# A scan layer's coefficients made in its projection phase, and block 0's spread weights picked out by TensorE

## The chip, the cores and the metric

The kernel runs on one core of one Trainium2 chip. The metric is the device time of one execution, in microseconds. Before the change the median of three runs is 3763.84 us (3762.84 to 3764.57).

## The reference

Four residual layers run one after the other on x (32 batches, 128 steps, 512 channels). Layers 1 and 2 are attention layers, which the change doesn't touch. Layers 0 and 3 are scan layers, each with weights of its own:

```
xr, gate = split(x @ W_in.T)                      # 1024 channels each
xc = silu(conv4(xr + t_emb) + b_conv)             # causal, one filter a channel
xn = layernorm(xc) * ln_g + ln_b
Bm, Cm, dt = split(xn @ W_xproj.T)                # 16 columns each
dt = tanh(dt @ W_dt.T + b_dt) * 0.01
Ad = 1 - dt * tanh(A_log)
Bd = Bm * minimum(norm(xn), 1)
h = clip(h * Ad[t] + Bd[t] * xn[t], -10, 10)      # 128 steps, 16 x 1024 a batch
y[t] = sum over the 16 states of Cm[t] * h
x = x + ((y + D * xn) * silu(gate)) @ W_out.T
```

## The kernel before

A scan layer is two phases with a barrier between them. Tiles named l0a and l3a belong to the projection phase of layers 0 and 3, l0r and l3r to the recurrence phase, l0s and l3s are kept over both. Inside a phase each engine works through its own instructions in order, and semaphores tie the engines together; SyncE (SP) and ScalarE (ACT) each have a queue of DMA issues of their own, and an issue that waits holds up all issues behind it on that engine.

**Projection (project_phase).** Eight tiles of four batches (512 tokens). SP loads W_in in 16 chunks of 512 columns; between the chunks it issues the small loads of a list, `loads`, one or two at a time. fold_dt (line 367, TensorE) multiplies W_dt into W_xproj as soon as all of `loads` have landed. VectorE evacuates the projected channels with t_emb added (line 616, tile l0a_pad), convolves them (line 627), and normalises; TensorE multiplies xn by W_xproj, and VectorE keeps the 48 columns of each token (line 658, l0s_proj). GpSimd makes the skip term D*xn (line 748), whose rows go to DRAM (dx_s); xn goes there split in a high and a low half (xhl_s), and so does the gate (gate_s). SP issues the last of these stores at line 286.

**Recurrence (recurrence_phase).** The state stands on 128 partitions of 8 batches x 16 states, for four groups of batches (GJ = 4), 1024 channels. A custom instruction of VectorE makes one step of one group (line 1196), so 512 make the scan; they are taken in 32 blocks of four steps. The recurrence is scaled by the running product `prod` of Ad: the feed is Bd/prod, the clip's bounds are 10/prod and -10/prod, and the reader's columns are Cm*prod. All that is made at the head of the phase, out of l0s_proj: VectorE removes the mean and applies the deviation for all 48 columns of all tokens in four products (lines 1155 to 1159), takes the three parts apart, waits for GpSimd's square root of the norms (line 911, a power), TensorE turns the parts so that steps lie along a row, ScalarE takes tanh, VectorE scans the product (line 1171), takes its reciprocal (1172), and makes the feed (1176), the bounds and the reader's columns. TensorE turns the feed back (line 996), ScalarE and VectorE split it (1100, 1180), and SP stores both halves to DRAM (feed_s, lines 844 and 846).

**Spread weights.** For each block SP loads the feed's rows from there, repeated over the partitions (line 852, l0r_crow, two loads of 256 KB a block), and GpSimd multiplies them by a mask `same` into block diagonal weights (line 922, l0r_wv). With those TensorE spreads xn over states and batches (line 1005, l0r_pv), the input of the steps. It reads a pair of steps out with the reader's columns (line 1020, l0r_py); ScalarE copies the sum out of PSUM (keep_y, line 1105, l0r_y), GpSimd adds the skip term and multiplies by the gate, and TensorE multiplies by W_out.

**Order at the recurrence's head.** SP issues x for blocks 0 and 1 (line 859, eight loads, which wait for the stores of the phase before), dx and gate of block 0, the feed's two stores, waits for both, then the spread rows of blocks 0 and 1, then W_out in eight chunks through two staging buffers (line 895): chunk c waits until chunk c-2 has been used. ScalarE casts a chunk (line 1125, l0r_woh), GpSimd makes its low half (line 970, l0r_wol). ScalarE's first keep_y comes behind the eight castings. TensorE's order for a pair of steps is spread, then read-out of the pair before; a read-out into l0r_py waits until ScalarE has copied the one before.

```
                        load_x(0, 0)
                        load_x(1, 1)
                        load_tokens(0, 0)
                        store_feed()
                        load_feed(0, 0)
                        load_feed(1, 1)
```

## Time and profile before

| what | value |
|---|---|
| median of three runs | 3763.84 us |
| the profiled execution | 3766.1 us |
| its span | 3764.3 us |
| mean granted TensorE clock | 0.963 |
| TensorE, VectorE busy | 3412.0 us (91%), 2965.0 us (79%) |
| GpSimd, ScalarE busy | 1868.6 us (50%), 1355.2 us (36%) |

The span is the time from the first to the last instruction of the profiled execution. The busy shares are means over layers that have different limits: the attention layers lie in the middle of the span, the scan layers at its ends. A timeline row gives the start from the span's start, the length, the engine (PE is TensorE, DVE VectorE, POOL GpSimd, SPq and ACTq the DMA issues of SyncE and ScalarE), the line, the operation, the tiles and how many equal instructions stand in the row; in brackets is how long the engine was idle before, and what released it.

### The profile page before, as it was taken

Reading aid. Unit: us, or ns where it says so; the run is one execution under the profiler, and the core shown is the slowest. Engines: PE = TensorE matmul, PEld = TensorE weight load, DVE = VectorE, ACT = ScalarE, POOL = GpSimd, SP = SyncE. Lnnn points to the kernel's source line nnn. Section 1 sums busy time; section 2 is a strip of 40 time slices with the busy share of each in tenths; the row PEclk is TensorE's granted clock in tenths of the full one; section 3 lists DMA queues with packets and bytes.
Section 4 is the critical chain, followed back from the end, with each engine's and each line's share of the span. In section 5 each row is a group of like instructions: output and inputs, shape, how many; then the busy total and the mean of one; then the engine's idle time right before and its main releaser. Section 6 shows DMA issues by size and latency. Waiting matters only on the chain. (4 is left out here: it accounts for less than half of the span.)

```text
span 3764.3 us, 62060 instructions
## 1 busy us (share of the span) xinstructions
PE 3412.0 (91%) x22068; PEld 2260.9 (60%) x22068; DVE 2965.0 (79%) x3172; ACT 1355.2 (36%) x2078; POOL 1868.6 (50%) x1384
## 2 busy tenths in 40 slices
PE   7999839999996899999999999997999948999998
PEld 6777614444443667777777777775777733444444
DVE  4777769999996777777778777763576769999998
ACT  3555512221222553444444444432455522122121
POOL 2555645655563024444454444433355655556554
PEclk9999959999998899999999999998999968999999
DMA  4566765565554224222322222224466675555553
GB/s 128 217 259 257 271 239 203 203 219 214 200 215 142 80 72 138 85 82 78 111 96 87 80 83 85 74 63 133 162 259 237 257 294 196 217 201 210 216 206 136
DMA packets 288573, 631.00 MB, mean 168 GB/s; under 512 B 33472, under 2 KB 35904, under 8 KB 288224
## 3 DMA queue, kind: packets, MB, share of 16 engines
q1 hardware_dynamic: 281200, 615.49, 46.6%
q10 hardware_dynamic: 7104, 11.81, 0.9%
q8 instruction: 183, 3.00, 0.3%
q14 instruction: 86, 0.70, 0.1%
HBM read 390.75 MB, written 241.70 MB: 168 GB/s over the span
## 5 line engine op out<-in xcount | busy, mean ns | idle before, releaser
L1196 DVE CUSTOM_DVE_ANT_0 l0r_g<-l0r_g,l0r_pv,l0r_cf 128x1024 f32<-128x1024 f32 x512 | 641.9, 1336 | 20.6 <-PE l0r_pv L1005 19.0
L1196 DVE CUSTOM_DVE_ANT_0 l3r_g<-l3r_g,l3r_pv,l3r_cf 128x1024 f32<-128x1024 f32 x512 | 641.8, 1337 | 17.8 <-PE l3r_pv L1005 16.2
L137 PE MATMUL l1h_ps_p<-l1h_xh,l1c_wh 128*128 128x512 f32 x768 | 323.3, 421 | 5.6 <-issue 3.3
L139 PE MATMUL l1h_ps_p<-l1h_xl,l1c_wh 128*128 128x512 f32 x768 | 306.3, 399 | 0.0
L138 PE MATMUL l1h_ps_p<-l1h_xh,l1c_wl 128*128 128x512 f32 x768 | 304.9, 397 | 0.0
L2182 POOL TENSOR_TENSOR l1h_st<-l1h_veps 128x1 f32<-128x1 f32 x64 | 35.4, 554 | 530.5 <-DVE l1h_veps L2040 530.5
L1794 ACT ACTIVATE l1h_pt<-l1h_ps_t 128x512 f32<-128x512 f32 x256 | 151.4, 591 | 330.7 <-PE l1h_ps_t L1667 330.7
L1020 PE MATMUL l0r_py<-l0r_g,l0r_cd 128*32 128x512 f32 x2048 | 253.1, 613 | 1.3 <-ACT l0r_y L1105 1.3
L1020 PE MATMUL l3r_py<-l3r_g,l3r_cd 128*32 128x512 f32 x2048 | 252.0, 611 | 0.8 <-ACT l3r_y L1105 0.8
L2080 DVE TENSOR_TENSOR l1h_e<-l1h_e,l1h_mx 128x1024 f32<-128x1024 f32 x128 | 207.2, 1619 | 4.4
L2099 DVE TENSOR_TENSOR l1h_vt<-l1h_ps_p,l1c_dc 128x512 f32<-128x512 f32 x64 | 44.3, 691 | 194.6 <-PE l1h_ps_p L139 194.6
L1005 PE MATMUL l0r_pv<-l0r_x,l0r_wv 32*128 32x512 f32 x1024 | 132.3, 503 | 50.6 <-DVE l0r_g L1196 29.7
L1787 ACT ACTIVATE l1h_e<-l1h_e 128x1024 f32<-128x1024 f32 x128 | 134.9, 1054 | 118.8 <-DVE l1h_e L2023 117.5
L1005 PEld LDWEIGHTS l0r_pv<-l0r_x,l0r_wv 32*128 32x128 f32 x1024 | 53.5, 185 | 206.3 <-issue 137.0
L1005 PE MATMUL l3r_pv<-l3r_x,l3r_wv 32*128 32x512 f32 x1024 | 131.4, 499 | 50.5 <-DVE l3r_g L1196 29.4
L1005 PEld LDWEIGHTS l3r_pv<-l3r_x,l3r_wv 32*128 32x128 f32 x1024 | 53.2, 184 | 205.8 <-issue 136.8
L627 DVE SCALAR_TENSOR_TENSOR l3a_pacc<-l3a_pad,l3a_wconv,l3a_pacc 128x512 f32<-128x512 f32 x192 | 144.8, 754 | 34.6 <-ACT l3a_pacc L485 30.1
L627 DVE SCALAR_TENSOR_TENSOR l0a_pacc<-l0a_pad,l0a_wconv,l0a_pacc 128x512 f32<-128x512 f32 x192 | 144.8, 754 | 34.1 <-ACT l0a_pacc L485 29.5
L2207 POOL TENSOR_TENSOR l1h_vl<-l1h_vt,l1h_vh 128x512 fp32r<-128x512 f32 x64 | 123.7, 1933 | 92.2 <-ACT l1h_vh L1825 92.2
L1667 PE MATMUL l1h_ps_t<-l1h_ident,l1h_e 128*128 128x128 f32 x1024 | 161.8, 281 | 6.4 <-ACT l1h_pt L1794 5.6
L139 PEld LDWEIGHTS l1h_ps_p<-l1h_xl,l1c_wh 128*128 128x128 f32 x768 | 145.9, 190 | 36.2
L137 PEld LDWEIGHTS l1h_ps_p<-l1h_xh,l1c_wh 128*128 128x128 f32 x768 | 146.4, 191 | 33.6 <-issue 4.3
(400 smaller groups left out, 8965.1 us busy)
## 6 DMA issues: line engine op xcount, KB each, us to landing
l0r_x<-xhl_s SPq DMA_DIRECT2D x128, 512.0 KB, 5.9
l3r_x<-xhl_s SPq DMA_DIRECT2D x128, 512.0 KB, 5.7
xhl_s<-l0a_xo SPq DMA_DIRECT2D x116, 512.0 KB, 4.6
xhl_s<-l3a_xo SPq DMA_DIRECT2D x116, 512.0 KB, 4.6
gate_s<-l0a_gate SPq DMA_DIRECT2D x64, 256.0 KB, 3.0
l0r_dx<-dx_s SPq DMA_DIRECT2D x32, 512.0 KB, 7.7
l0r_gate<-gate_s SPq DMA_DIRECT2D x32, 512.0 KB, 8.6
l0r_crow<-feed_s SPq DMA_DIRECT2D x64, 256.0 KB
```

Of the source, the lines that this page charges most:

```text
L137: pe.matmul(out, wh, xh, start=first, stop=False)
L138: pe.matmul(out, wl, xh, start=False, stop=False)
L139: return pe.matmul(out, wh, xl, start=False, stop=last)
L627: dve.scalar_tensor_tensor(out=a, in0=pad[:, it % 2, :, c:c + S], scalar=wconv[:, it, c:c + 1], in1=a, op0=ALU.mult, op1=ALU.add).then_inc ...
L1005: last = pe.matmul(pv[(k.off + t + 2 * p + a) % 3][:, h * HALF:(h + 1) * HALF], wv[r, k.parity(), 2 * t + p, :], x[r, k.parity(), t, p, :] ...
L1020: last = pe.matmul(py[j * JW:(j + 1) * JW, :], cd[:, k.parity(), t, j, at:at + JW], g[:, t, j, h * HALF:(h + 1) * HALF], start=t % 2 == 0 ...
L1196: dve._custom_dve(bass.dve_ops.TENSOR_ADD_SAT, out=g[:, t, j, :], in0=g[:, (t - 1) % TS, j, :], in1=pv[(k.off + t + j) % 3][:, :], s0=cf[: ...
L1667: last = pe.transpose(ps_t[:, h * S:(h + 1) * S], e[:, k.mod(2), u // 2, h, u % 2, :], ident[:, :])
L1787: act.activation(e[:, k.mod(2), half, :, :, :], e[:, k.mod(2), half, :, :, :], ACT.Exp).then_inc(exp_ok, 1)
L1794: act.activation(pt[:, u % 2, :, :], ps_t[:, :].rearrange("p (h s) -> p h s", h=HG), ACT.Copy).then_inc(pt_ok, 1)
L2080: dve.tensor_tensor(block, block, total.unsqueeze(3).to_broadcast([P, HG, 2, S]), ALU.mult).then_inc(en_ok, 1)
L2207: pool.tensor_tensor(vl[:, n.mod(2), :, :], vt[:, n.parity(), :, b * S:(b + 1) * S], vh[:, n.mod(2), :, :].bitcast(F32), ALU.subtract).the ...
```

## The change

Three things move, in both scan layers.

- **The coefficients.** Normalising the columns of dt and of Bm, turning them, tanh, the running product, its reciprocal and the feed are made at the end of the projection phase. The feed and the product are kept in `carry`, a tile that takes the place of l0a_pad; the intermediate values stand in the projection's xc tile. The columns of dt come first, then those of Bm; those of Cm stay in the recurrence. GpSimd's square root of the norms is split in 28 columns, between its last two skip terms, and 4 behind the last one.
- **The constants.** same, ymask, A_log and a new array `comb` are kept over both phases and are loaded by SP as the last four of `loads`; ScalarE's loads at the recurrence's head are gone, and so is the second load of ident.
- **Block 0's weights.** The spread rows of block 0 are no longer loaded. GpSimd makes two tiles of picks from comb and ident; TensorE multiplies the split feed by them in 16 matmuls, and VectorE multiplies the sum by `same`. The feed's store to DRAM and block 1's load remain. Rows of even blocks now come into `carry`, those of odd blocks into l0r_crow. GpSimd clears g in place of VectorE.

```diff
+                 (drow[:, :], w["D"].partition_broadcast(P)),
+                 (same[:, :], cst["same"]),
+                 (ymask[:, :], cst["ymask"]),
+                 (comb[:, :], cst["comb"]),
+                 (alog[:, :], w["A_log"].rearrange("(a n b) -> a n b", a=1, b=1).to_broadcast([GB, NS, 1]))]
...
+            for c, part in enumerate((steps, gains)):
+                pe.wait_ge(ready, c + 1)
+                for j in range(GJ):
+                    last = pe.transpose(ptr[:, c * TW + j * S:c * TW + (j + 1) * S], part[:, j * P:(j + 1) * P], ident[:, :])
+                last.then_inc(swung, 1)
...
+            act.wait_ge(summed, 1)
+            act.activation(acol[:, 0:1], alog[:, :], ACT.Tanh).then_inc(tanh, 1)
+            act.wait_ge(swung, 1)
+            act.activation(decay.rearrange("p j s -> p (j s)"), ptr[:, 0:TW], ACT.Tanh).then_inc(tanh, 1)
...
+            def normalise(c, m, out):
+                cols = slice(c * NS, (c + 1) * NS)
+                chain(dve.tensor_tensor(m, stat[:, :, 0].unsqueeze(2).to_broadcast(wide),
+                                        wsum[:, cols].unsqueeze(1).to_broadcast(wide), ALU.mult))
+                chain(dve.tensor_tensor(m, proj[:, :, cols], m, ALU.subtract))
+                chain(dve.tensor_tensor(m, m, stat[:, :, 2].unsqueeze(2).to_broadcast(wide), ALU.mult))
+                return dve.tensor_tensor(out, m, wbias[:, cols].unsqueeze(1).to_broadcast(wide), ALU.add)
...
+            dve.wait_ge(proj_ev, NT)
+            dve.wait_ge(rstd, B)
+            normalise(2, means[0], steps.rearrange("p (b n) -> p b n", b=B)).then_inc(ready, 1)
+            rows_b = gains.rearrange("p (b n) -> p b n", b=B)
+            chain(normalise(0, means[1], rows_b))
+            dve.wait_ge(root, 2)
+            chain(dve.tensor_scalar(norm[:, :], norm[:, :], 1.0, None, ALU.min))
+            dve.tensor_tensor(rows_b, rows_b, norm[:, :].unsqueeze(2).to_broadcast(wide), ALU.mult).then_inc(ready, 1)
+            chain(dve.memset(zero, 0.0))
+            dve.wait_ge(tanh, 2)
+            chain(dve.tensor_scalar(acol[:, 1:2], acol[:, 0:1], -0.01, None, ALU.mult))
+            chain(dve.tensor_scalar(decay, decay, acol[:, 1:2], 1.0, ALU.mult, ALU.add))
+            for j in range(GJ):
+                chain(dve.tensor_tensor_scan(prod[:, j, :], decay[:, j, :], zero, 1.0, ALU.mult, ALU.add))
+            inv = proj[:, :, 0:NS]
+            chain(dve.reciprocal(inv, prod.rearrange("p j (a b) -> p (j a) b", b=NS)))
+            dve.wait_ge(swung, 2)
+            chain(dve.tensor_tensor(feed.rearrange("p j (a b) -> p (j a) b", b=NS), ptr[:, TW:2 * TW].rearrange("p (a b) -> p a b", b=NS),
+                                    inv, ALU.mult))
...
+            def lengths(lo, hi):
+                pool.wait_ge(ss, hi)
+                pool.tensor_tensor(norm[:, lo:hi], stat[:, lo:hi, 3], half[:, :].to_broadcast([P, hi - lo]), ALU.pow).then_inc(root, 1)
...
                 if n >= B - TB:
                     skip_term(n)
+                if n == B - 2:
+                    pool.wait_ge(summed, 1)
+                    pool.memset(half[:, :], 0.5).then_inc(halved, 1)
+                    pool.wait_ge(halved, 2)
+                    lengths(0, B - TB)
+            lengths(B - TB, B)
...
+        rows_of_feed = (carry[:, 0:2 * TS * P].rearrange("p (a i) -> p a i", i=P), crow[:, :, :])
+        PICK = P + HALF_P
+        picks = [z.rearrange("p e m i -> p (e m i)")[0:32, GJ * P:GJ * P + PAIR * PICK].rearrange("p (t n) -> p t n", t=PAIR) for z in (zh, zl)]
...
-                at_least(sp, wvm, k - 1)
+                at_least(sp, wvm, k - 2)
+                if q == 0 and isinstance(k, int):
+                    sp.wait_ge(coefs, 3)
                 for h in range(2):
-                    sp.dma_start(crow[h * 64:(h + 1) * 64, q, :, :].rearrange("p a i -> p (a i)"),
+                    sp.dma_start(rows_of_feed[q][h * 64:(h + 1) * 64, :, :].rearrange("p a i -> p (a i)"),
...
                         store_feed()
-                        load_feed(0, 0)
                         load_feed(1, 1)
...
-            pool.memset(half[:, :], 0.5).then_inc(root, 1)
-            pool.wait_ge(root, 1)
-            pool.tensor_tensor(norm[:, :], stat[:, :, 3], half[:, :].to_broadcast([P, B]), ALU.pow).then_inc(root, 1)
-            for r in range(2):
-                pool.wait_ge(sent[1][r], 64 * B // 2)
+            for c in range(2):
+                pool.tensor_tensor(picks[c], comb[:, :].unsqueeze(1).to_broadcast([32, PAIR, PICK]),
+                                   ident[0:32, PAIR * c:PAIR * c + PAIR].unsqueeze(2).to_broadcast([32, PAIR, PICK]), ALU.mult).then_inc(pick, 1)
+            for q in range(2):
+                pool.wait_ge(sent[1][q], 64 * B // 2)
+                pool.wait_ge(sent[2][q], 16 * B // 2)
             pool.memset(cd[:, :, :, :, :], 0.0).then_inc(zeroed, 1)
+            pool.memset(g[:, TS - 1, :, :], 0.0).then_inc(gup, GJ)
             pool.wait_ge(zeroed, 1)
-            pool.wait_ge(same_ld, 32)
-            pool.wait_ge(step, 8 + 3 + GJ + 1 + 3)
+            pool.wait_ge(coefs, 3)
...
                         bounds(0, 0)
-                        weigh(0, 0, 1)
                         readers(0, 0)
                     if not (last and q == 1):
                         bounds(k + 1, 1 - q)
-                        weigh(k + 1, 1 - q, i + 1 + q)
+                        weigh(k + 1, 1 - q, i + 1)
...
-            pe.wait_ge(const, 16)
-            pe.wait_ge(step, 8)
-            for c in range(3):
-                for j in range(GJ):
-                    last = pe.transpose(pt[c][:, j * S:(j + 1) * S], parts[c][:, j * P:(j + 1) * P], ident[:, :])
-            last.then_inc(turned, 1)
-            pe.wait_ge(fed, 1)
             for j in range(GJ):
                 last = pe.transpose(pf[:, (j % 2 * 2 + j // 2) * P:(j % 2 * 2 + j // 2 + 1) * P], feed[:, j, :], ident[:, :])
             last.then_inc(feed_turned, 1)
+            pe.wait_ge(read_ready, 1)
+            for j in range(GJ):
+                last = pe.transpose(pc[:, j * S:(j + 1) * S], reads[:, j * P:(j + 1) * P], ident[:, :])
+            last.then_inc(read_turned, 1)
+            pe.wait_ge(pick, 2)
+            for c, half in enumerate((feed_h, feed_l)):
+                pe.wait_ge((feed_high, feed_low)[c], 1)
+                for t in range(TS):
+                    for e in range(2):
+                        last = pe.matmul(pv[2][:, t * 2 * P:(t + 1) * 2 * P], picks[t // PAIR][:, t % PAIR, HALF_P - 32 * e - 16 * c:HALF_P - 32 * e - 16 * c + P], half[0:32, 2 * e:2 * e + 2, :],
+                                         start=c == e == t % 2 == 0, stop=c == e == t % 2 == 1)
+            last.then_inc(picked, 1)
...
-                pe.wait_ge(wvm, k.count(1, 1))
+                at_least(pe, wvm, k.count())
+                if k.is_at(0):
+                    pe.wait_ge(first_w, 1)
...
-            act.dma_start(ident[:, :], cst["ident"]).then_inc(const, 16)
-            for b in range(GB):
-                act.dma_start(alog[b * NS:(b + 1) * NS, :], w["A_log"].rearrange("(n a) -> n a", a=1)).then_inc(alog_ld, 16)
-            act.dma_start(same[:, :], cst["same"]).then_inc(same_ld, 16)
-            act.dma_start(ymask[:, :], cst["ymask"]).then_inc(same_ld, 16)
-            act.wait_ge(alog_ld, 16 * GB)
-            act.activation(acol[:, 0:1], alog[:, :], ACT.Tanh).then_inc(tanh, 1)
-            act.wait_ge(turned, 1)
-            act.activation(decay.rearrange("p j s -> p (j s)"), pt[2], ACT.Tanh).then_inc(tanh, 1)
...
-            full = [P, B, NPROJ]
-            chain(dve.tensor_tensor(mean_w, stat[:, :, 0].unsqueeze(2).to_broadcast(full),
-                                    wsum[:, :].unsqueeze(1).to_broadcast(full), ALU.mult))
...
-            dve.tensor_tensor(feed, turn[0], inv, ALU.mult).then_inc(fed, 1)
...
+            inv, scale = proj[:, :, 0:NS].rearrange("p (j a) b -> p j a b", j=GJ), coef[:, 2, :, :].rearrange("p s j -> p j s")
+            for c, bound in enumerate((CLIP, -CLIP)):
+                dve.tensor_scalar(coef[:, c, :, :].rearrange("p (a b) j -> p j a b", b=NS), inv, bound, None, ALU.mult).then_inc(coefs, 1)
             dve.wait_ge(feed_high, 1)
             dve.tensor_tensor(feed_l.rearrange("s j i -> s (j i)"), pf, feed_h.bitcast(F32).rearrange("s j i -> s (j i)"),
                               ALU.subtract).then_inc(feed_low, 1)
-            chain(dve.tensor_scalar(out[1], inv, -CLIP, None, ALU.mult))
-            dve.wait_ge(sent[2][1], 16 * B // 2)
-            dve.memset(g[:, TS - 1, :, :], 0.0).then_inc(gup, GJ)
+            wide, cols = [P, B, NS], slice(NS, 2 * NS)
+            m = mean_w.rearrange("p (b n) -> p b n", b=B)
+            chain(dve.tensor_tensor(m, stat[:, :, 0].unsqueeze(2).to_broadcast(wide),
+                                    wsum[:, cols].unsqueeze(1).to_broadcast(wide), ALU.mult))
+            chain(dve.tensor_tensor(m, proj[:, :, cols], m, ALU.subtract))
+            chain(dve.tensor_tensor(m, m, stat[:, :, 2].unsqueeze(2).to_broadcast(wide), ALU.mult))
+            dve.tensor_tensor(reads.rearrange("p (b n) -> p b n", b=B), m, wbias[:, cols].unsqueeze(1).to_broadcast(wide), ALU.add)\
+               .then_inc(read_ready, 1)
+            dve.wait_ge(picked, 1)
+            dve.tensor_tensor(wv[:, 0, :, :], pv[2][:, :].rearrange("p (a i) -> p a i", a=2 * TS),
+                              same[:, :].unsqueeze(1).to_broadcast([P, 2 * TS, P]), ALU.mult).then_inc(first_w, 1)
+            dve.wait_ge(read_turned, 1)
+            dve.tensor_tensor(scale, pc.rearrange("p (j s) -> p j s", j=GJ), prod, ALU.mult).then_inc(coefs, 1)
```

At the end of layer 0's projection and the head of its recurrence GpSimd (POOL) has this order before (l0a_xt takes a skip term, l0r_norm the norms, l0r_cd the reader's columns, l0r_cf the coefficients of a block):

```order
L748 TENSOR_TENSOR l0a_xt<-l0a_xn,l0a_drow 128x1024 x2
L45 UNCONDITIONAL_BRANCH
L47 ISA
L907 UNCONDITIONAL_BRANCH
L909 MEMSET l0r_half 128x1
L911 TENSOR_TENSOR l0r_norm<-l0s_stat,l0r_half 128x32
L914 MEMSET l0r_cd 128x1568
L927 COPY l0r_cf<-l0s_coef 128x48
L922 TENSOR_TENSOR l0r_wv<-l0r_crow,l0r_same 128x1024
L934 TENSOR_TENSOR l0r_cd<-l0r_ymask,l0r_cf 128x16x8
```

And this after the change (the norms stand in a part of l0a_ones, the picks in l0r_zh and l0r_zl):

```order
L812 TENSOR_TENSOR l0a_xt<-l0a_xn,l0a_drow 128x1024
L841 MEMSET l0a_ones 128x1
L821 TENSOR_TENSOR l0a_ones<-l0s_stat,l0a_ones 128x28
L812 TENSOR_TENSOR l0a_xt<-l0a_xn,l0a_drow 128x1024
L821 TENSOR_TENSOR l0a_ones<-l0s_stat,l0a_ones 128x4
L45 UNCONDITIONAL_BRANCH
L47 ISA
L975 UNCONDITIONAL_BRANCH
L978 TENSOR_TENSOR l0r_zh<-l0s_comb,l0s_ident 32x384
L978 TENSOR_TENSOR l0r_zl<-l0s_comb,l0s_ident 32x384
L983 MEMSET l0r_cd 128x1568
L984 MEMSET l0r_g 128x4096
```

The power has moved in front of the barrier, the larger part of it between the two skip terms; block 0's product with `same` has left GpSimd.

At the start of layer 0's projection SP's queue has this order before, from the last load of the list on:

```order
L314 DMA l0a_drow<-L_D 128x1024
L301 DMA l0a_stage<-L_W_inC 128x512 x9
L269 DMA l0a_xt<-xT 128x4x512
L277 DMA gate_s<-l0a_gate 64x2x512 x8
L269 DMA l0a_xt<-xT 128x4x512
```

And after the change:

```order
L332 DMA l0a_drow<-L_D 128x1024
L332 DMA l0s_same<-same 128x128
L319 DMA l0a_stage<-L_W_inC 128x512
L332 DMA l0s_ymask<-ymask 128x8
L332 DMA l0s_comb<-comb 32x192
L319 DMA l0a_stage<-L_W_inC 128x512
L332 DMA l0s_alog<-L_A_log 128x1x1
L319 DMA l0a_stage<-L_W_inC 128x512 x7
```

Four small loads stand among the chunks of W_in, the last of them behind the ninth chunk; all of them belong to the list for which fold_dt waits.

At the head of layer 0's recurrence SP has this order before (l0r_wst is the staging of W_out):

```order
L859 DMA l0r_x<-xhl_s 128x1024 x8
L865 DMA l0r_dx<-dx_s 128x2x512
L865 DMA l0r_gate<-gate_s 128x2x512
L844 DMA feed_s<-l0r_zh 128x2x256
L846 DMA feed_s<-l0r_zl 128x2x256
L852 DMA l0r_crow<-feed_s 64x1x1024 x4
L895 DMA l0r_wst<-L_W_outT 128x512 x8
L852 DMA l0r_crow<-feed_s 64x1x1024 x2
```

And after the change:

```order
L928 DMA l0r_x<-xhl_s 128x1024 x8
L934 DMA l0r_dx<-dx_s 128x2x512
L934 DMA l0r_gate<-gate_s 128x2x512
L911 DMA feed_s<-l0r_zh 128x2x256
L913 DMA feed_s<-l0r_zl 128x2x256
L921 DMA l0r_crow<-feed_s 64x1x1024 x2
L963 DMA l0r_wst<-L_W_outT 128x512 x8
L921 DMA l0s_carry<-feed_s 64x1x1024 x2
```

One pair of spread-row loads is gone from in front of W_out; the rest stands as it did.

## Rows read from the trace of the kernel before

**Rows 1.** VectorE's timeline, layer 0's recurrence; start, us, instruction, count, [idle before, releaser].

```profile
525.81 10.10 DVE L1196 CUSTOM_DVE_ANT_0 l0r_g<-l0r_g,l0r_pv,l0r_cf 128x1024 f32<-128x1024 f32 x8 [12.76 <-PE l0r_pv L1005]
...
563.96 611.59 DVE L1196 CUSTOM_DVE_ANT_0 l0r_g<-l0r_g,l0r_pv,l0r_cf 128x1024 f32<-128x1024 f32 x488 [1.64 <-PE l0r_pv L1005]
```

**Rows 2.** Timeline of all engines at layer 0's read-out of block 0.

```profile
545.13 0.58 ACT L1105 ACTIVATE l0r_y<-l0r_py 128x512 f32<-128x512 f32 x1
...
545.85 3.64 PE L1020 MATMUL l0r_py<-l0r_g,l0r_cd 128*32 128x512 f32 x16 [1.32 <-ACT l0r_y L1105]
```

**Rows 3.** Timeline of all engines, end of layer 0's projection and next phase's start.

```profile
474.11 6.63 POOL L748 TENSOR_TENSOR l0a_xt<-l0a_xn,l0a_drow 128x1024 f32<-128x1024 f32 x2
...
478.46 0.34 DVE L658 COPY l0s_proj<-l0a_pp 128x192 f32<-128x192 f32 x1
...
480.68 2.73 SPq L286 DMA_DIRECT2D xhl_s<-l0a_xh  x2
...
484.77 1.76 DVE L1155 TENSOR_TENSOR l0r_g<-l0s_stat,l0s_wsum 128x1536 f32<-128x1536 f32 x1 [5.97 <-PEq L48]
484.91 6.91 POOL L911 TENSOR_TENSOR l0r_norm<-l0s_stat,l0r_half 128x32 f32<-128x32 f32 x1
...
495.15 3.72 SPq L859 DMA_DIRECT2D l0r_x<-xhl_s  x8
```

**Rows 4.** Timeline of all engines, layer 0: spread rows and the first of W_out.

```profile
513.04 2.65 SPq L852 DMA_DIRECT2D l0r_crow<-feed_s  x4
...
522.38 2.34 POOL L922 TENSOR_TENSOR l0r_wv<-l0r_crow,l0r_same 128x1024 fp32r<-128x1024 f32 x1 [13.38 <-DMA l0r_crow<-feed_s]
...
527.84 2.35 POOL L922 TENSOR_TENSOR l0r_wv<-l0r_crow,l0r_same 128x1024 fp32r<-128x1024 f32 x1 [2.60 <-DMA l0r_crow<-feed_s]
528.37 1.28 ACT L1125 ACTIVATE l0r_woh<-l0r_wst 128x512 fp32r<-128x512 f32 x2 [21.08 <-DMA l0r_wst<-L_W_outT]
```

**Rows 5.** Timeline of all engines, the same places of layer 3.

```profile
3096.71 2.34 POOL L922 TENSOR_TENSOR l3r_wv<-l3r_crow,l3r_same 128x1024 fp32r<-128x1024 f32 x1 [13.28 <-DMA l3r_crow<-feed_s]
...
3101.75 2.36 POOL L922 TENSOR_TENSOR l3r_wv<-l3r_crow,l3r_same 128x1024 fp32r<-128x1024 f32 x1 [2.17 <-DMA l3r_crow<-feed_s]
...
3120.01 3.64 PE L1020 MATMUL l3r_py<-l3r_g,l3r_cd 128*32 128x512 f32 x16 [0.81 <-ACT l3r_y L1105]
...
3135.70 611.39 DVE L1196 CUSTOM_DVE_ANT_0 l3r_g<-l3r_g,l3r_pv,l3r_cf 128x1024 f32<-128x1024 f32 x488 [0.96 <-PE l3r_pv L1005]
```

**Rows 6.** Timeline, VectorE's coefficients of layer 0.

```profile
492.87 0.18 DVE L1164 TENSOR_SCALAR l0r_norm<-l0r_norm 128x32 f32<-128x32 f32 x1
...
498.85 0.15 DVE L1168 TENSOR_SCALAR l0r_acol<-l0r_acol 128x1 f32<-128x1 f32 x1 [4.82 <-ACT l0r_g L1098]
...
504.79 0.69 DVE L1176 TENSOR_TENSOR l0r_g<-l0r_pv,l0r_g 128x512 f32<-128x512 f32 x1
```

**Rows 7.** Windows: us, busy us of engines, granted TensorE clock, DMA share, GB/s.

```profile
476.00:494.00 18.00, 0.00 (x0) 0.00 (x0) 11.33 (x11) 1.37 (x3) 11.74 (x4) 0.50 1.04 387
496.00:511.00 15.00, 3.22 (x14) 2.42 (x12) 10.64 (x13) 1.40 (x3) 0.69 (x2) 0.50 1.01 376
```

**Rows 8.** Timeline of all engines, start of layer 0's projection.

```profile
29.52 1.95 PE L367 MATMUL l0a_pp<-l0a_wdt,l0a_dx 16*128 16x16 f32 x16 [1.60 <-DMA l0a_drow<-L_D]
30.22 0.33 SPq L301 DMA_DIRECT2D l0a_stage<-L_W_inC  x1
...
36.05 0.69 DVE L616 TENSOR_TENSOR l0a_pad<-l0a_pxr,l0a_temb 128x512 f32<-128x512 f32 x1 [1.55 <-PE l0a_pxr L139]
...
41.53 2.34 DVE L627 SCALAR_TENSOR_TENSOR l0a_pacc<-l0a_pad,l0a_wconv,l0a_pacc 128x512 f32<-128x512 f32 x3 [1.32 <-ACT l0a_pacc L485]
...
45.87 0.76 PE L137 MATMUL l0a_pg<-l0a_wih,l0a_xh 128*128 128x512 f32 x1 [4.27 <-DVE l0a_pad L616]
```

**Rows 9.** DMA issues from 484 to 496: queue, count, KB each, us to landing.

```profile
l0r_alog<-L_A_log ACTq DMA_DIRECT2D x8, 0.1 KB, 6.5
...
l0r_ymask<-ymask ACTq DMA_DIRECT2D x1, 4.0 KB, 2.4
```

93 lines of the change are left out of this document (42 added, 51 removed).

## The prediction

> **What bounds the kernel now.** I read first the timeline of VectorE in layer 0's recurrence. One instruction makes a step, 512 of them, and from the 25th on (563.96) 488 run in 611.59 us without a gap, 1.253 us each [rows 1]. Nothing of the change is in there, so what can move is the stretch from the end of the projection to that point, twice, in layers 0 and 3. The first step starts at 525.81; at 1.253 us a step the 25th would be due at 555.9, and it comes at 563.96, so 8 us of the entry are lost after the first step. The timeline of the entry says where. TensorE's read-out of block 0's last pair of steps but one (line 1020, 545.85) was released by ScalarE's copy of y (line 1105, 545.13) [rows 2]. That copy stands in ScalarE's queue behind the eight castings of W_out (line 1125), and TensorE, whose queue is in order, can't give block 1 its products before that read-out. So block 1 hangs on W_out, and W_out hangs on a long chain: first load of x (495.15), 5.2 MB of x, dx and gate, the feed's two stores behind them on the same queue, the spread rows (line 852, 513.04), W_out's first chunk (528.37), then the loop of load, ScalarE and GpSimd up to the last casting, right in front of the copy at 545.13 [rows 2 to 4]. In before this chain and the steps arrive within 1.3 us of each other: read-out waited 1.32 us for the copy.
>
> **The change, part by part.** I follow the W_out chain through it, since making the first step earlier only lets TensorE wait longer at that same read-out.
>
> (a) One pair of spread-row loads less. In before block 0's pair is served first (GpSimd starts its product at 522.38), block 1's lands 5.46 us later (527.84), and W_out's first chunks 0.5 us after that (528.37): they wait behind the second pair. In layer 3 the two products start at 3096.71 and 3101.75, 5.04 us apart [rows 4, 5]. With block 0 made by TensorE the pair for block 1 is the first, so everything behind it comes 5.5 us (layer 0) and 5.0 us (layer 3) sooner, counted from the moment the feed is stored. Bounds: 0 if the single pair lands no earlier than two did, 7 if without the other it also lands sooner itself. I take the rows' value.
>
> (b) The projection's phase ends later. GpSimd has two skip products of 3.32 us each from 474.11; between them now come a fill and the power of 28 columns, behind them that of 4. The power of 32 columns took 6.91 us, 0.216 a column, so 6.05 and about 1.0 (a little over 0.86 for the start of an instruction) [rows 3]. 474.11 + 3.32 + 0.2 + 6.05 + 3.32 + 1.0 = 488.0. VectorE starts its new work at 478.8 and has eight products of 128x512, some 0.75 each with the gap (0.69 in the row of line 1176), until 484.8; so it waits for GpSimd. Steps' transposes and tanh lie beside that. Then clamp, product and fill, 1.17 (492.87 until 498.85 less 4.82 idle), and from the A column to the feed 6.63 (498.85 to 504.79 + 0.69), 7.8 in all [rows 6]: 495.8. SyncE's last issue ended at 483.41 and the next phase began at 484.77, 1.36 later: 497.1 for the first x, where before it was 495.15, since those loads waited for the stores and not for the engines [rows 3]. The cost is 1.9 us a layer. Bounds: 0 if the stores still end last, 4 if the last dx row, whose store is issued some 6 us later than before, ends last itself. The queue is full in these stretches, 387 GB/s up to 494 and 376 from 496 to 511 [rows 7], so the feed's store still ends when x, dx and gate have gone, 17.9 us after the first x issue (495.15 to 513.04), however early it is issued. Layer 3 I take the same.
>
> (c) The start of the projection. Folding W_dt (line 367) waits for all of `loads`, and there are 13 now instead of 9. The 13th, A_log, is issued behind the ninth chunk of W_in, whose issue is at 30.22, so at about 30.6; a small load landed in 2.4 us [rows 8, 9]. That makes 33.2 with the issue, where fold started at 29.52: 3.7 us of delay for TensorE. VectorE was waiting for TensorE right behind it (1.55 us at 36.05), so it takes the delay over, and gives back only its next wait for ScalarE (1.32 at 41.53). TensorE in turn waits 4.27 us at 45.87 for VectorE's last evacuation of this block [rows 8]. So 3.7 - 1.3 = 2.4 us of the phase are lost, and behind it TensorE has no such pause until the phase's last block. Bounds: 0 if the load lands by 31, 7 if it takes the 6.5 us that the A_log rows took on ScalarE's queue [rows 9].
>
> (d) What I cost at nothing. GpSimd's picks (two of 32x384) and its memset of g (VectorE's work in before), the picks' 16 matmuls, VectorE's product for block 0 and the four products of the C columns all lie between 497 and some 510, and what they release, block 0, has until the read-out at about 544. Should W_out go from the path, they would be the next to count. The four loads of constants that ScalarE issued at the head of the recurrence had nothing behind them on the path but the tanh, which goes into the projection's tail under GpSimd's power. Block 1's product on GpSimd is still in front of W_out's low halves, as before.
>
> Sum: layer 0, 2.4 + 1.9 - 5.5 = -1.2; layer 3, 2.4 + 1.9 - 5.0 = -0.7; together -1.9 us. What follows the read-out I take as before: 18.1 us to the 25th step in layer 0 (545.85 to 563.96), 15.7 in layer 3 (3120.01 to 3135.70) [rows 1, 2, 5]. TensorE's granted clock is 0.50, its lower level of 1.2 GHz, in the stretches of the entry [rows 7], and the read-out's 16 matmuls take 3.64 us in both layers. TensorE will have idled some 15 us there, so each layer may fall to either figure, 2.4 us up or down. The profiled execution took 3766.1, its span 3764.3 and 1.8 around it; it becomes 3764.2. The median of the timed runs is 2.3 lower, 3763.84, and that becomes 3761.9.
>
> One rule of the Trainium skill speaks against (b). Row first: in the recurrence's entry the power of 32 columns ran on GpSimd from 484.91 to 491.82, and VectorE's first product, with two inputs from SBUF, ran beside it from 484.77 in 1.76 us for 1536 columns, no slower than three of 512 at 0.69 [rows 3, 6]. The Trainium skill, "SBUF — State Buffer", "SBUF: two separate sides", says that a VectorE instruction with two SBUF inputs and a GpSimd instruction that reads SBUF exclude each other for the whole instruction. By that rule the new products of 512 columns would wait for the power of 28 columns. The trace does not bear that out.
>
> **The rivals.** (1) The first step decides after all, because the castings of W_out come early enough. The entry would then shorten by all that the first step gains: the phase at 497.1 + 2.4, transposes, copy, low half and picks some 5 (an estimate: 20 short matmuls, and two instructions of 512 columns at 0.69 [rows 6]), product and TensorE's first matmuls 3.4 (522.38 to 525.81), so 508 instead of 525.8 [rows 1, 4]; 17.8 us a layer, 3728. Against it stands the copy's place in ScalarE's queue, and the chain that I found no way around. (2) The 13th load is hidden and the single pair of spread rows lands 1.5 us sooner than the first pair did: 2.4 + 1.5 more a layer, 3754. (3) Slower: the 13th load lands late. Its source has eight rows of 16 single elements, and the eight A_log loads of before took 6.5 us [rows 9]. Fold would start at 37.5, the phase lose 8.0 - 1.3 = 6.7, and a layer come out 3.1 to 3.6 us longer: 3770.5. It decides from a landing of 3.2 us on, where (c) and (b) together reach the 5.25 of (a); the clock at its lower level in both layers makes it 3773. (4) GpSimd's power holds up VectorE. The eight products would start at 483.7 and end, between skip product and last power, near 491.5 instead of 488.0: 3.5 us a layer, 3769. It is the rule above as a mechanism of this kernel.
>
> **How the numbers follow.** My forecast, no change to speak of, gets 0.58; (1) 0.06; (2) 0.17; (3) 0.13; (4) 0.06. Differences below 0.2%, 7.5 us, can't be told from none here. Faster by more: (1), (2) and a little of the forecast's lower edge, 0.24. Slower by more: the part of (3) and (4) in which TensorE's clock also stays low, and 0.04 for the forecast's upper edge, 0.16. Within: 0.60. The forecast's own range is 3757 to 3767, from the clock's 2.4 either way and half of the bounds in (b) and (c). The whole one goes from 3752, which takes in (2), to 3771, which takes in most of (3) and (4).
>
> **What would show it.** In the profile after: fold (line 367 before) starting 3 to 4 us later and released by A_log; GpSimd with the power of 28 columns between the two skip products and VectorE idle until 488 to 491; the first x issue 4 us later in layer 0; VectorE's first step near 509; TensorE idle some 15 us or more before the read-out of block 0's second pair, released by ScalarE's copy of y, and that read-out near 545. I am wrong if VectorE's steps run from the first on without that pause, or if fold does not wait.

## The result, and the profile after

The changed kernel takes 3775.94 us (median of 6 runs, 3773.75 to 3780.69) where before takes 3764.2 (6 runs, 3762.48 to 3770.74): ratio 1.0030, 95% interval 1.0017 to 1.0043. It is slower by 11.7 us, and the time lies outside the range forecast. The profiled execution took 3776.21, its span 3774.4 (before 3766.1 and 3764.3), at a mean granted clock of 0.961 (0.963).

Page of the changed kernel: span, then busy time, share and count by engine.

```profile
span 3774.4 us, 62104 instructions
...
PE 3431.9 (91%) x22100; PEld 2275.7 (60%) x22100; DVE 2980.3 (79%) x3184; ACT 1355.0 (36%) x2078; POOL 1865.9 (49%) x1390
```

The shares are those of before to a percent; where the time went is seen by stages. First the start of layer 0's projection, to be laid beside [rows 8] (start, length, engine, line, tiles, count, [idle, releaser]):

```profile
31.18 0.34 SPq L319 DMA_DIRECT2D l0a_stage<-L_W_inC  x1
31.56 0.78 SPq L332 DMA_DIRECT2D l0s_alog<-L_A_log  x1
...
35.24 3.59 PE L385 MATMUL l0a_pp<-l0a_wdt,l0a_dx 16*128 16x16 f32 x16 [6.62 <-DMA l0s_alog<-L_A_log]
...
43.99 0.69 DVE L643 TENSOR_TENSOR l0s_carry<-l0a_pxr,l0a_temb 128x512 f32<-128x512 f32 x1 [8.29 <-PE l0a_pxr L139]
...
48.02 2.32 DVE L654 SCALAR_TENSOR_TENSOR l0a_pacc<-l0s_carry,l0a_wconv,l0a_pacc 128x512 f32<-128x512 f32 x3
...
50.82 1.43 POOL L792 TENSOR_TENSOR l0a_wil<-l0a_stage,l0a_wih 128x512 fp32r<-128x512 f32 x1 [2.13 <-ACT l0a_wih L500]
51.05 1.62 DVE L693 TENSOR_TENSOR l0a_wxb<-l0a_wx,l0a_bcol 128x384 f32<-128x384 f32 x1
...
53.41 0.51 PE L137 MATMUL l0a_pg<-l0a_wih,l0a_xh 128*128 128x512 f32 x1 [3.86 <-DVE l0s_carry L643]
```

The fold waits for A_log, as forecast, but starts 5.7 us late instead of 3.7, and then takes 3.59 us instead of 1.95. VectorE's evacuation comes 7.9 us late (43.99 for 36.05). TensorE's pause before the gate's first matmul is nearly as long as before (3.86 for 4.27), and the gate starts 7.5 us late (53.41 for 45.87).

The end of the projection and the head of the recurrence, all engines, beside [rows 3, 4]:

```profile
481.41 3.33 POOL L812 TENSOR_TENSOR l0a_xt<-l0a_xn,l0a_drow 128x1024 f32<-128x1024 f32 x1
...
484.86 5.62 POOL L821 TENSOR_TENSOR l0a_ones<-l0s_stat,l0a_ones 128x28 f32<-128x28 f32 x1
...
488.31 0.69 DVE L766 TENSOR_TENSOR l0a_xc<-l0a_xc,l0s_wbias 128x512 f32<-128x512 f32 x1
...
490.46 2.79 POOL L812 TENSOR_TENSOR l0a_xt<-l0a_xn,l0a_drow 128x1024 f32<-128x1024 f32 x1
491.09 2.71 DVE L766 TENSOR_TENSOR l0a_xc<-l0a_xc,l0s_wbias 128x512 f32<-128x512 f32 x1
493.21 1.46 POOL L821 TENSOR_TENSOR l0a_ones<-l0s_stat,l0a_ones 128x4 f32<-128x4 f32 x1
494.77 0.18 DVE L774 TENSOR_SCALAR l0a_ones<-l0a_ones 128x32 f32<-128x32 f32 x1 [0.98 <-POOL l0a_ones L821]
...
503.74 8.24 DVE L1222 TENSOR_SCALAR l0s_coef<-l0s_proj 128x512 f32<-128x512 f32 x2 [1.26 <-PEq L48]
503.89 4.56 SPq L928 DMA_DIRECT2D l0r_x<-xhl_s  x8
...
521.47 1.27 SPq L921 DMA_DIRECT2D l0r_crow<-feed_s  x2
...
530.93 2.37 POOL L991 TENSOR_TENSOR l0r_wv<-l0r_crow,l0s_same 128x1024 fp32r<-128x1024 f32 x1 [7.54 <-DMA l0r_crow<-feed_s]
531.42 1.27 ACT L1191 ACTIVATE l0r_woh<-l0r_wst 128x512 fp32r<-128x512 f32 x2 [25.96 <-DMA l0r_wst<-L_W_outT]
```

The reader sees the tail of GpSimd (skip product, 28 columns, skip product, 4 columns) and VectorE behind it, as described. From the first issue of x to that of the spread rows it is 17.58 us (17.89 before), and one pair of rows is loaded, not two: W_out's first casting comes 27.53 us behind the first x, before 33.22. Layer 3 and the read-out tell the same:

```profile
548.48 0.58 ACT L1171 ACTIVATE l0r_y<-l0r_py 128x512 f32<-128x512 f32 x1
549.20 3.31 PE L1093 MATMUL l0r_py<-l0r_g,l0r_cd 128*32 128x512 f32 x16 [5.84 <-ACT l0r_y L1171]
...
3110.53 2.37 POOL L991 TENSOR_TENSOR l3r_wv<-l3r_crow,l3s_same 128x1024 fp32r<-128x1024 f32 x1 [13.44 <-DMA l3r_crow<-feed_s]
3111.12 1.28 ACT L1191 ACTIVATE l3r_woh<-l3r_wst 128x512 fp32r<-128x512 f32 x2 [26.22 <-DMA l3r_wst<-L_W_outT]
...
3128.81 3.64 PE L1093 MATMUL l3r_py<-l3r_g,l3r_cd 128*32 128x512 f32 x16 [11.74 <-ACT l3r_y L1171]
```

TensorE waits 5.84 and 11.74 us for ScalarE's copy of y (1.32 and 0.81 before, [rows 2, 5]): W_out's chain is the bound, and the steps have slack. VectorE's steps:

```profile
522.91 10.10 DVE L1250 CUSTOM_DVE_ANT_0 l0r_g<-l0r_g,l0r_pv,l0r_cf 128x1024 f32<-128x1024 f32 x8 [0.55 <-POOL l0r_cf L996]
...
559.27 616.39 DVE L1250 CUSTOM_DVE_ANT_0 l0r_g<-l0r_g,l0r_pv,l0r_cf 128x1024 f32<-128x1024 f32 x492 [0.96 <-PE l0r_pv L1078]
...
3148.31 608.89 DVE L1250 CUSTOM_DVE_ANT_0 l3r_g<-l3r_g,l3r_pv,l3r_cf 128x1024 f32<-128x1024 f32 x486 [0.16 <-issue]
```

The first of these long rows begins with the 21st step, so the 25th starts at 559.27 + 4 x 1.253 = 564.28, 0.3 later than before. The row in layer 3 begins with the 27th; the 25th starts at 3145.55, 9.85 later than before [rows 5].

The stages between these rows, in us against before:

| stage | layer 0 | layer 3 | forecast |
|---|---|---|---|
| start of the projection, to GpSimd's last two skip terms | +7.3 | +6.5 | +2.4 each |
| its end, to the first x | +1.4 | +1.1 | +1.9 each |
| first x to W_out's first casting | -5.7 | -4.6 | -5.5, -5.0 |
| castings | +0.3 | 0 | 0 |
| read-out to the 25th step | -3.0 | +1.1 | 2.4 either way |
| from layer 0's last step to layer 3's first load | +5.7 | | nothing |

They sum to 10.1, which is the difference of the spans. Two rows depart from the forecast: the first, where the forecast is too small by 9.0 us in all, and the last, in two layers that the change does not touch. Each stage is read from one execution, and equal instructions differ from profile to profile: from the fold to the first x, e10 below took 469.9 us and e12, equal up to there, 465.5. A term that matters is therefore taken from several kernels, in the last part.

The last row is seen in TensorE's timeline at one run of score matmuls (the two attention layers have 67 such runs of 32), of before, and then of after:

```profile
1579.09 1.17 PE L1654 MATMUL l1h_ps_s<-l1h_kt,l1h_qt 32*128 32x128 f32 x32 [0.61 <-issue]
...
1582.52 0.47 PE L137 MATMUL l1h_ps_p<-l1c_wh,l1h_vh 128*128 128x512 f32 x1 [1.67 <-issue]
```

```profile
1580.26 0.94 PE L1708 MATMUL l1h_ps_s<-l1h_kt,l1h_qt 32*128 32x128 f32 x21 [0.47 <-issue]
...
1583.32 1.22 PE L1708 MATMUL l1h_ps_s<-l1h_kt,l1h_qt 32*128 32x128 f32 x11 [2.13 <-issue]
```

In before the 32 score matmuls run in one piece, and the pause of 1.67 us in which TensorE waits for nothing that the profile shows lies behind them. In after it is 2.13 us and lies inside them, after the 21st, so VectorE's softmax, which needs all 32, waits as well. The windows show what follows (stretch, its length in us, busy us of PE, PEld, DVE, ACT, POOL, granted clock, DMA share, GB/s), of after:

```profile
1580.00:1585.00 5.00, 2.61 (x35) 2.20 (x36) 0.94 (x2) 0.00 (x0) 0.00 (x0) 0.79 0.02 3
1585.00:1590.00 5.00, 5.00 (x15) 3.98 (x14) 3.20 (x2) 1.65 (x2) 0.00 (x0) 0.53 0.01 3
```

and of before:

```profile
1580.00:1585.00 5.00, 3.33 (x27) 2.54 (x20) 3.52 (x2) 1.48 (x2) 0.00 (x0) 1.00 0.02 3
```

Behind the pause the granted clock of after falls towards its lower level (0.53 of full speed, 0.5 being 1.2 GHz), and before stays at 2.4 GHz. From the start of this run to TensorE's next wait of this kind (3.3 us, at 1889.12 in before and 1893.93 in after) after loses 3.6 us. Layer 2 has a like pause in after alone (1.82 us at 2223.81), and 1.8 us more are lost from there on. TensorE's waits of this kind sum to 8.2 us over the attention layers of after, to 6.4 in before.

In the same ten microseconds the DMA view of after, by queue (packets, MB, share), has instructions moving:

```profile
q8 instruction: 2, 0.03, 1.4%
```

The Trainium skill, "Runtime: NRT & Kernel Launch", "Instruction fetch mechanics", says that instructions are refilled in blocks of 16 KiB in order, and that crossing from one block into the next is mostly hidden. Two packets of 0.03 MB fit such refills; that crossing is hidden does not fit the pause, if a crossing is what it is, which no row names. In before this queue moved three packets, 0.05 MB, around its own pause (1575 to 1585), so the packets don't tell the two kernels apart.

### The profile page after: what moved, and what is told of

Same layout as the page of the kernel before. It is cut to its first block and busy times, and to the rows that moved or that the text cites. A ratio compares the mean times of both kernels' runs of the same rounds, so it can differ in the third digit from the quotient of the medians.

```text
span 3774.4 us, 62104 instructions
## 1 busy us (share of the span) xinstructions
PE 3431.9 (91%) x22100; PEld 2275.7 (60%) x22100; DVE 2980.3 (79%) x3184; ACT 1355.0 (36%) x2078; POOL 1865.9 (49%) x1390
## 5 line engine op out<-in xcount | busy, mean ns | idle before, releaser
L1093 PE MATMUL l3r_py<-l3r_g,l3r_cd 128*32 128x512 f32 x2048 | 254.0, 615 | 11.7 <-ACT l3r_y L1171 11.7
L654 DVE SCALAR_TENSOR_TENSOR l3a_pacc<-l3s_carry,l3a_wconv,l3a_pacc 128x512 f32<-128x512 f32 x192 | 144.7, 754 | 30.2 <-ACT l3a_pacc L508 25.6
L654 DVE SCALAR_TENSOR_TENSOR l0a_pacc<-l0s_carry,l0a_wconv,l0a_pacc 128x512 f32<-128x512 f32 x192 | 144.7, 754 | 30.1 <-ACT l0a_pacc L508 25.5
L2068 DVE TENSOR_REDUCE l1h_mx<-l1h_ps_s 128x16 f32<-128x2048 f32 x64 | 146.5, 2289 | 22.3 <-PE l1h_ps_s L1708 22.3
L138 PEld LDWEIGHTS l1h_ps_p<-l1h_xh,l1c_wl 128*128 128x128 f32 x768 | 146.9, 191 | 27.3
```

The lines of the kernel that those rows point to most:

```text
L138: pe.matmul(out, wl, xh, start=False, stop=False)
L654: dve.scalar_tensor_tensor(out=a, in0=pad[:, it % 2, :, c:c + S], scalar=wconv[:, it, c:c + 1], in1=a, op0=ALU.mult, op1=ALU.add).then_inc ...
L1093: last = pe.matmul(py[j * JW:(j + 1) * JW, :], cd[:, k.parity(), t, j, at:at + JW], g[:, t, j, h * HALF:(h + 1) * HALF], start=t % 2 == 0 ...
L2068: dve.reduce_max(mx[:, k.mod(2), :, :], ps_s[:, :].rearrange("p (h u s) -> p h u s", h=HG, u=TB), AX.X)\
```

## The experiments

Two theories for the loss stood at the outset: the wait of the fold for the 13th load (F), and something that the picks or the feed's new way cost in the entry (P). The place of TensorE's program in the attention layers (A) came up with the first results. Every ratio is to runs of before on the same chip, and brackets hold its 95% interval; the times of different rows can come from different chips. The last three columns are read from one execution each: those of e1 (3757.54) and e12 (3730.50) are the fastest of theirs, those of e10 (3751.33) and e14 (3758.71) the slowest.

| kernel | us (runs) | ratio to before | fold | 25th step, layer 0 | last step of layer 0 to layer 3's first load of x |
|---|---|---|---|---|---|
| before | | 1 | 29.52 | 563.96 | 1392.95 |
| after | 3775.94 (6) | 1.0030 [1.0017, 1.0043] | 35.24 | 564.28 | 1398.68 |
| e1 | 3765.55 (11) | 1.0001 [0.9992, 1.0010] | 30.28 | 556.88 | 1396.21 |
| e2 | 3780.09 (5) | 1.0036 [1.0022, 1.0050] | 34.99 | 567.34 | 1391.30 |
| e3 | 3767.58 (11) | 1.0007 [0.9998, 1.0016] | 34.32 | 558.12 | 1397.40 |
| e4 | 3771.87 (11) | 1.0015 [1.0006, 1.0024] | 30.25 | 563.85 | 1393.73 |
| e5 | 3755.37 (5) | 0.9961 [0.9948, 0.9974] | 30.35 | 551.14 | 1401.53 |
| e6 | 3775.14 (11) | 1.0020 [1.0011, 1.0028] | 33.20 | 562.31 | 1397.75 |
| e7 | 3775.35 (11) | 1.0018 [1.0009, 1.0026] | 33.77 | 564.44 | 1397.82 |
| e8 | 3760.72 (12) | 0.9986 [0.9977, 0.9995] | 29.20 | 559.93 | 1390.02 |
| e10 | 3745.48 (5) | 0.9937 [0.9924, 0.9951] | 29.66 | 551.65 | 1399.04 |
| e11 | 3775.48 (8) | 1.0024 [1.0013, 1.0035] | 30.85 | 560.93 | 1400.66 |
| e12 | 3733.24 (5) | 0.9911 [0.9897, 0.9924] | 29.39 | 543.18 | 1391.26 |
| e13 | 3768.02 (11) | 1.0006 [0.9997, 1.0015] | 33.96 | 563.45 | 1391.79 |
| e14 | 3754.88 (6) | 0.9968 [0.9956, 0.9980] | 30.08 | 559.25 | 1390.53 |
| e15 | 3767.19 (11) | 1.0000 [0.9991, 1.0009] | 29.45 | 561.72 | 1390.81 |

**e1, the four constants counted apart.** The last four loads get a semaphore of their own, and only ScalarE's tanh waits for it.

```diff
-                 (drow[:, :], w["D"].partition_broadcast(P)),
-                 (same
+                 (drow[:, :], w["D"].partition_broadcast(P))]
+        late_loads = [(same
...
+            act.wait_ge(late, 16 * len(late_loads))
             act.activation(acol
```

> The changed kernel, with same, ymask, comb and A_log counted on a semaphore of their own that ScalarE waits for ahead of its tanh; fold waits for the nine old loads alone. Theory (A_log's late landing is the loss): fold starts at 29.5 to 30.5 us again instead of 35.2, the recurrence's first x issue comes 7 us sooner in layer 0 and 5 in layer 3, and the time falls by 8 to 12 us, to 3764 to 3768. Rival (the loss sits in the recurrence's entry, in VectorE's 8.24 us pair of bounds products beside GpSimd's memset of g): fold moves, but the 25th step stays within 2 us a layer, 3772 to 3776. Rival (the loss is in the attention layers, which stand at other places of the program): no more than 2 us a scan layer, and the attention layers take 1385 us again.

The fold is back, released by the D rows as in before [rows 8]:

```profile
30.28 1.95 PE L388 MATMUL l0a_pp<-l0a_wdt,l0a_dx 16*128 16x16 f32 x16 [1.98 <-DMA l0a_drow<-L_D]
```

The ratio goes from 1.0030 to 1.0001. That names F, and takes nearly all of the loss with it, though the attention layers are still 3.3 us longer than in before: what the rest of the change saves and what A costs nearly cancel here, as e14 shows below.

**e7, A_log first in the list.** Is it A_log's shape that lands late, or its place?

```diff
+        loads = [(alog[:, :], w["A_log"]...to_broadcast([GB, NS, 1])), (gcol[:, :], w["ln_gT"]),
...
-                 (alog[:, :], w["A_log"]...to_broadcast([GB, NS, 1]))]
```

> The changed kernel, with A_log as the first instead of the last of the 13 loads that fold waits for, so that comb's is the last. Theory (fold waits for A_log's late issue and landing, not for the number of loads): fold at 30.3 to 31.5 us in layer 0, as with the constants counted apart, and 3764 to 3768. Rival (any load behind the chunks of W_in is as late): fold at 33 to 35, 3770 to 3775.

```profile
30.86 0.33 SPq L319 DMA_DIRECT2D l0a_stage<-L_W_inC  x1
31.23 0.43 SPq L332 DMA_DIRECT2D l0s_comb<-comb  x1
...
33.77 3.59 PE L385 MATMUL l0a_pp<-l0a_wdt,l0a_dx 16*128 16x16 f32 x16 [6.30 <-DMA l0s_comb<-comb]
```

Now comb is the last, issued behind the ninth chunk, and the fold starts 2.5 us behind its issue (33.77 less 31.23). With A_log there it was 3.7 in after and 3.1 to 3.8 in e2, e3, e6 and e13. A_log's shape is worth 0.5 to 1.3 us, the place the rest of the delay, and the time is that of after: any 13th load in that place is late.

**e2, block 0 from DRAM as before.** The picks are taken out, the rest of the change stays.

```diff
+                        load_feed(0, 0)
                         load_feed(1, 1)
...
-            for c in range(2):
-                pool.tensor_tensor(picks[c], comb..., ident..., ALU.mult).then_inc(pick, 1)
```

> The changed kernel, with block 0's weights made as before: its spread rows loaded from DRAM ahead of block 1's and weighed by GpSimd, no picks. Theory (one pair of spread rows less in front of W_out is worth 5 us a layer): W_out's first casting comes 15 us behind the spread rows' issue instead of 10, the read-out of block 0's second pair 5 us later, and the time rises by 6 to 10 us, to 3782 to 3786. Rival (the pair was hidden): the read-out stays, 3775 to 3777.

W_out's first casting goes from 531.42 to 534.32, and the 25th step from 564.28 to 567.34, in layer 0; from the first load of layer 3 to its 25th step, 7.9 us are lost. So the picks are worth 11 us up to the 25th steps of these profiles, and P falls. But the time is only 4.2 us above that of after (2.3 by the ratios): without layer 0's 16 picks ahead of them, the attention layers are 7.4 us shorter. That is below the 3782 to 3786 that I expected, and the first sign of A.

**e6, the power in eight pieces.** GpSimd's 28 columns are spread over the phase, four at a time.

```diff
-                if n == B - 2:
+                if n == TB:
...
+                if n % TB == TB - 1 and TB < n < B - 1:
+                    lengths(n - 2 * TB + 1, n - TB + 1)
```

> The changed kernel, with the power of the norms taken in eight pieces of four columns over the batches of the projection, so that 4 instead of 28 columns stand between GpSimd's last two skip terms. Theory (GpSimd's power delays the phase's end): the recurrence's first x issue comes 2 to 3.5 us sooner against the start of its phase's last skip terms, and the time falls by 3 to 6 us, to 3770 to 3773. Rival (the phase's end is bound by the stores that drain): the first x issue moves by less than 1 us, 3775 to 3777.

From the last skip terms to the first x it is 21.97 us instead of 22.48. No gain: with GpSimd out of the way, VectorE's own chain ends the phase there.

**e3 and e4, W_out early.** ScalarE's queue loads W_out whole into g at the phase's head; the eight castings wait for nothing behind the feed. e3 is this on after, e4 on before.

```diff
-        wst = ph.sb("wst", [P, 2, DM])
+        wst = g[:, 2, :, :].rearrange("p j (e n) -> p (j e) n", n=DM)
...
+            for h in range(2):
+                act.dma_start(wst[:, 4 * h:4 * h + 4, :], w_out[:, 4 * h:4 * h + 4, :]).then_inc(w_ld[h], 16)
```

> The changed kernel, with W_out loaded by ScalarE's queue at the recurrence's head into a free part of g, all eight chunks at once, and cast and halved there, ahead of block 0's bounds. Theory (the W_out chain sets the entry): the read-out of block 0's second pair no longer waits for ScalarE's copy, the steps run from about 523 to 528 without a pause longer than 2 us, the 25th starts at 553 to 559 instead of 564.3, and the time falls by 10 to 20 us, to 3756 to 3766. Rival (TensorE's low clock or block 1's spread rows take the wait over): a pause of 6 us or more stays before the 25th step, 3771 to 3776.

> The kernel before, with W_out loaded at the recurrence's head in the same way as in the run on the changed kernel. Theory (the W_out chain sets the entry here too): the first step at 526 to 531, the 25th at 556 to 561 instead of 564, the time falls by 6 to 16 us, to 3748 to 3758. Rival (chain and steps arrived together, so other waits of the same length stand behind it): within 3 us of the kernel before, 3761 to 3767.

On after it brings 6.2 us in layer 0 and some 8 in all, less than the 10 to 20 that I expected; it shows that the chain through W_out was the bound there. On before it costs: 2 MB in front of the feed's store put the spread rows' issue from 513.04 to 518.31 and the first step from 525.81 to 530.21. The 25th step of layer 0 stays (563.85 for 563.96): what the steps gain without the wait for W_out goes into their late start. In layer 3 the 25th comes 3.0 us later behind the layer's first load of x. My expectation of e4 was wrong, its rival too. What W_out releases was not gained here, where the feed's store stands behind it.

**e8, e4 with the loads of block 1's x, dx and gate behind the spread rows.**

```diff
                         load_x(0, 0)
-                        load_x(1, 1)
-                        load_tokens(0, 0)
                         store_feed()
                         load_feed(0, 0)
                         load_feed(1, 1)
+                        load_x(1, 1)
+                        load_tokens(0, 0)
```

> The kernel before, with W_out early as in the run on it, and x of block 1, dx and gate issued behind the spread rows. Theory (the bytes queued in front of the feed's store set the spread rows, and these the first step; early W_out alone put 2 MB more there): the spread rows are issued at 509 to 512 us instead of 518.3, first step at 521 to 525, 25th at 555 to 559, and the time is 6 to 14 us below the kernel before, 3751 to 3760. Rival (TensorE at its lower clock sets it anyway): the 25th step stays at 562 to 564, 3763 to 3768.

The rows' issue is back at 513.2, not before, and the first step at 526.18; I had expected 509 to 512 and 521 to 525. The 25th step comes 4 us sooner than in before; a small gain, just above the upper edge of what I expected.

**e5 and e10, all of it on after.** e5 is e1, W_out early, the order of e8, g cleared by VectorE, and GpSimd's picks held until VectorE's bounds are made. e10 puts block 0's bounds and reader between the fourth and the fifth low half.

```diff
+            for c in range(KI // 2):
+                low_out(c)
...
                         bounds(k + 1, 1 - q)
+                        if first and q == 0:
+                            for c in range(KI // 2, KI):
+                                low_out(c)
```

> The changed kernel with four edits: the four constants counted apart from the loads that fold waits for; W_out loaded all at once at the recurrence's head by ScalarE's queue and cast ahead of block 0's bounds; x of block 1, dx and gate issued behind the spread rows; g cleared by VectorE, and GpSimd's picks behind VectorE's two bounds products. Theory (what sets the 25th step is the later of the first step + 34 us and the last casting of W_out + 16 us; the first step hangs on the bytes queued in front of the feed): first step at 514 to 519, 25th at 549 to 553 in layer 0, 11 to 15 us sooner than before, as much in layer 3: 3736 to 3746. Rival (a wait not seen yet, such as GpSimd's low halves in front of the bounds, takes over): the first step at 522 or later, 3755 to 3765.

> The kernel with the four edits together, with GpSimd's bounds of blocks 0 and 1 and the reader's columns moved between the fourth and the fifth low half of W_out; VectorE waits for all low halves at the step that first overwrites W_out's staging. Theory (in that kernel the first step waits 8 us for GpSimd's low halves): first step at 511 to 513 instead of 517.6 in layer 0, the 25th at 545 to 547 instead of 551.1, and 3743 to 3750. Rival (TensorE's lower clock at the start keeps the 25th step where it is): 3753 to 3757.

VectorE in e5:

```profile
497.06 1.09 DVE L1226 TENSOR_SCALAR l0s_coef<-l0s_proj 128x512 f32<-128x512 f32 x2 [1.26 <-PEq L48]
...
517.61 10.11 DVE L1256 CUSTOM_DVE_ANT_0 l0r_g<-l0r_g,l0r_pv,l0r_cf 128x1024 f32<-128x1024 f32 x8 [7.92 <-POOL l0r_cf L1000]
```

The two products of the bounds take 1.09 us with GpSimd held, 8.24 in after beside the picks and the clears; in e2, without the picks, they take 1.10. The first step waits 7.92 us for GpSimd's bounds behind eight low halves, the rival of that expectation; e10 takes that away (2.02 us left) and is at 3745.48. The first step comes at 514.09, but the 25th of layer 0 not sooner than in e5 (551.65 for 551.14), where I had expected 545 to 547; layer 3's comes 3.1 us sooner behind the layer's first load of x.

**e11, e13, e14, e15 and e12, the place alone.** Inert matmuls of 16 columns at the start of TensorE's attention program, whose result nobody reads: 16 on before (e11, as many as the picks of layer 0), 48 on after (e13) and on e1 (e14), 64 on before (e15), 48 on e10 (e12).

```diff
             pe.wait_ge(const, 32)
+            for _ in range(16):
+                pe.matmul(ps_p[0][0:16, 0:16], ident[:, 0:16], ident[:, 0:16], start=True, stop=True)
```

> The kernel before, with 16 more matmuls of 16 columns at the start of the attention layers' TensorE program, in time that TensorE waits anyway, so that all its later instructions stand where the change's 16 picks of layer 0 push them. Theory (the attention layers' 5 us come from the place of TensorE's program, where it waits for nothing that the profile shows): these waits sum to about 8 us in the attention layers instead of 6, the layers take 1396 to 1400 us instead of 1390 to 1394, and the time is 4 to 6 us above the kernel before. Rival (they are chance, or come with a shifted start): 1390 to 1394 us, within 2 us of the kernel before.

> The changed kernel with 48 inert matmuls of 16 columns at the start of the attention layers' TensorE program, which makes 64 more than in the kernel before, with the change's 16. Theory (the place of TensorE's program costs the changed kernel 6 to 8 us): attention layers at 1390 to 1394 us instead of 1398.7, and 3766 to 3770, so 0 to 4 us above the kernel before, which is what the scan layers lose. Rival (the place is not it in this kernel): 3774 to 3778.

> The changed kernel with the constants counted apart and the same 48 matmuls. Theory (two separate causes, fold's wait and the place, which add up): 3756 to 3760, 6 to 10 us below the kernel before. Rival (with fold early the place matters no more, or the other way round): 3763 to 3767.

> The kernel before with 64 of these matmuls, so that its attention layers stand at the same place as in the other two. Theory (it is a place as good as the kernel before has): attention layers at 1389 to 1394 us, 3763 to 3768. Rival (more than the number of TensorE's instructions decides): 1396 us or more, 3770 to 3776.

> The kernel with the bounds moved ahead of the low halves, with 48 such matmuls at the start of the attention layers. Theory (place of TensorE's program): the attention layers' time changes by 3 us or more against the same kernel without the 48, either way. Rival (chance): it stays within 2 us of it.

TensorE at the same run of scores, in e11 and then in e13:

```profile
1575.12 0.49 PE L1656 MATMUL l1h_ps_s<-l1h_kt,l1h_qt 32*128 32x128 f32 x5 [0.90 <-issue]
...
1577.72 2.07 PE L1656 MATMUL l1h_ps_s<-l1h_kt,l1h_qt 32*128 32x128 f32 x27 [2.10 <-issue]
```

```profile
1579.68 1.17 PE L1710 MATMUL l1h_ps_s<-l1h_kt,l1h_qt 32*128 32x128 f32 x32 [0.69 <-issue]
```

Before with 16 matmuls gets the pause inside the run, after the fifth and not after the 21st, so the 16 don't put the program quite where the change puts it. It loses 9 us by the ratio, more than the 4 to 6 that I expected; after with 48 more, 64 in all, has them in one piece and gains 8. The work itself is not it: with 64 on before the time is that of before, ratio 1.0000. The windows of e13 stay at full clock where those of after fell to 0.53:

```profile
1580.00:1585.00 5.00, 5.00 (x55) 4.20 (x48) 3.84 (x3) 0.89 (x2) 0.00 (x0) 1.00 0.00 0
1585.00:1590.00 5.00, 5.00 (x38) 3.79 (x37) 4.58 (x9) 3.68 (x6) 2.10 (x3) 1.00 0.27 70
```

Taken over all sixteen profiles: in the eight where a pause parts this run of 32 (after, e1, e3, e5, e6, e7, e10, e11) the stretch of the table's last column takes 1396.21 to 1401.53 us, in the eight where it goes in one piece 1390.02 to 1393.73; the means are 7.1 us apart. So A is shown as far as the place goes. That the pause is a fetch of instructions is argued from the queue's packets and not shown. e14 comes out at 3754.88, under the 3756 to 3760 that I expected for two causes that add up. e12 is the best version: 3733.24 us, ratio 0.9911. It is 12.2 us below e10, of which the attention layers explain 7.8; layer 0's first x, behind equal instructions in both, comes 4.8 us sooner in the profile of e12, which stays open (one profile is the slowest execution of its kernel, the other the fastest).

## Why the prediction was wrong

**The chain.** Right. Block 1 hangs on W_out in after too (5.84 and 11.74 us of waiting for the copy of y), and rival (1) falls. TensorE's wait was not the 15 us or more that I named as a sign, since the first step, which I had seen near 509, came at 522.91 (see (d)).

**(a)** Right: -5.7 and -4.6 for -5.5 and -5.0, and the 17.9 us from first x to spread rows held (17.58, 17.93).

**(b)** Right in the mechanism and the sum: +1.4 and +1.1 for 1.9. The rule of the Trainium skill that I weighed there ("SBUF — State Buffer", "SBUF: two separate sides") did not bite beside the power: the products of 512 columns that ran beside the 28 columns took 0.69. One beside the second skip product took 2.71 (491.09, its end that of the skip product within 0.6), which fits the rule; it lay inside VectorE's wait for the last power. Rival (4) falls: VectorE's products were not held for 3.5 us.

**(c)** Here the working failed; the term was mis-sized, 7.3 and 6.5 us in these two profiles for 2.4. Over all sixteen profiles, from the phase's first load of x to GpSimd's last two skip terms, the six kernels whose fold waits for a 13th load take 4.9 us longer in the mean than the ten others in layer 0, and 5.0 in layer 3 (from their spread, an estimate, some 0.5 uncertain). The timed runs allow more: counting the constants apart is worth 11 us (e1 against after, by the ratios) and 14 (e14 against e13), 5 to 7 a layer. Its three parts:

- The delay. In layer 0 the fold starts at 33.20 to 35.24 in the six kernels (mean 34.25), and at 29.20 to 30.85 in the ten others (mean 29.9): 4.3 where I had 3.7. In layer 3, counted from the phase's first load of x, it is 3.3. So the 3.7 was right in the mean, though put together otherwise: the load was issued about 31 instead of 30.6, and the fold followed 3.1 to 3.8 behind the issue where I took 2.6.
- The clock. TensorE idled 6.62 us in front of the fold, and the granted clock went to its lower level. Windows of after, and then of before, from the fold on:

```profile
35.00:39.00 4.00, 3.76 (x17) 3.73 (x18) 0.70 (x1) 2.53 (x4) 1.96 (x3) 0.50 0.40 112
39.00:43.00 4.00, 4.00 (x10) 3.13 (x11) 0.00 (x0) 1.11 (x2) 1.95 (x2) 0.50 0.46 128
```

```profile
29.00:33.00 4.00, 3.48 (x21) 3.15 (x22) 2.22 (x4) 1.98 (x4) 2.46 (x2) 0.86 0.32 87
33.00:37.00 4.00, 4.00 (x14) 3.18 (x13) 2.19 (x4) 2.46 (x4) 2.56 (x2) 0.71 0.52 125
```

  The fold alone took 1.64 us more, and its matmuls behind it 0.6, so a fold that starts 5.7 us late makes VectorE's evacuation 7.9 us late. In the first window VectorE has 0.70 us of work, in the second none. I had looked for the clock in the entry and put these 2.2 us at nothing here.
- What is given back. I subtracted 1.3 us, a wait of VectorE for ScalarE, as slack. That wait is gone in after (48.02, no idle before it), and VectorE is 6.5 us late there instead of 7.9. But its product l0a_wxb, a little later, takes 1.62 us; in before it took

```profile
44.58 0.55 DVE L666 TENSOR_TENSOR l0a_wxb<-l0a_wx,l0a_bcol 128x384 f32<-128x384 f32 x1
```

  In after GpSimd had begun its product for W_in (50.82) when VectorE began this one (51.05). Of the 32 such products of VectorE, two in each of the sixteen profiles, the eleven that began while GpSimd's was running took 1.62 to 1.65 us and the others 0.54 to 0.55. So 1.1 us are lost again, and the gate starts 7.5 us late.

So the delay and the slack came out as worked, and the step that failed is what was put at nothing between fold and gate: the 2.2 us of the low clock and the 1.1 us of the product. In the mean the six kernels take 1.7 us longer from fold to gate in both layers, where the sum had 1.3 less.

The nearest rival was (3), 3770.5: it was to decide from a landing of 3.2 us on, and 3.1 to 3.8 was found, so its place and sign were right, without the 6.5 us that it was priced by.

**(d)** Nothing was lost by it, but it was not where I had put it. The first step comes 19.0 us behind the first x in layer 0 (522.91 less 503.89), not some 10: VectorE's products of the bounds take 8.24 us beside GpSimd's picks and clears, in front of the feed's low half and the picks' matmuls. The wait for W_out's chain covered that: 5.84 us of it were still left.

**What was left out.** I looked for no cost outside the two scan layers. The 16 picks in layer 0 move all of TensorE's later instructions, and the attention layers lost 5.7 us by it. The one trace of it in before is TensorE's pause of 1.67 us behind that run of scores, released by nothing, which I had not read.

e13 and e15 both have 64 matmuls more than before ahead of the attention layers. Between them the change costs 0.8 us by the medians (3768.02 and 3767.19) and 2.3 by the ratios, no change that can be told: forecast and range would have held there. With the constants counted apart the change saves 12 us at that place (e14 and e15, 0.9968 and 1.0000). So the wrong size of (c), some 2.6 us a layer by the profiles, cost the forecast the sign of its sum, and the place put the time beyond the range.

## What to carry to other kernels

Before adding a load to a list that one semaphore counts, ask which instruction waits for the whole count, and when the last of the list is issued behind what: a constant that is needed 450 us later cost the head of the phase some 5 us. Where a stage that a change doesn't touch gets longer, look for "issue" waits of the engine whose instructions moved, and shift them with a few inert ones before blaming the change. Where two chains meet within 1.3 us, a gain in one is seen only when the other is shortened as well, and a transfer taken from one chain can be put in front of the other (e4).

## What was not expected of the hardware

- The same two attention layers take 7 us more or less by where TensorE's program stands: a pause of 2.1 us behind the 5th or the 21st matmul of one run of 32, with the granted clock falling to 0.65 and 0.53, against 1.67 us behind the 32nd or none, at full clock.
- Two tensor_scalar instructions of VectorE (one input each) took 8.24 us beside GpSimd's picks and clears, 1.10 without the picks (e2) and 1.09 with GpSimd held (e5). A product with two inputs took 1.62 instead of 0.55 when a product of GpSimd had begun before it, and 0.55 when it began first.
- The power on GpSimd isn't in proportion to its columns: 28 took 5.62 us (0.20 each), 4 took 1.46 (0.37 each).
- A small load behind a bulk chunk let its reader start 2.5 (comb) and 3.1 to 3.8 us (A_log) after its issue.
